# Transposing attention probabilities in halves of 64 query rows, with a reciprocal moved between minima and a store bound set once

## The chip, the core and the metric

The kernel runs on one core of one Trainium2 chip. The metric is the device time of one execution in microseconds (us); lower is better. The core's engines run their own instruction streams and meet at semaphores: TensorE (PE: matmuls, and PEld: its weight loads), VectorE (DVE), ScalarE (ACT), GpSimd (POOL) and SyncE (SP, which issues transfers). TensorE writes to PSUM, eight banks of 512 fp32 values on each of 128 partitions; VectorE and ScalarE copy from there to SBUF.

## The reference

Everything is fp32. `x` is (2, 512, 256), the context (2, 1024, 256). Two gated residual steps:

```
x = x + tanh(g_xattn) * (softmax(mask(q k^T / 8)) v) @ Wo + bo     # q = layernorm(x) @ Wq; k, v = ctx @ Wk, ctx @ Wv
x = x + tanh(g_ffn) * FFN_e(layernorm(x))                          # e = argmax(layernorm(x) @ Wg + bg), 8 experts
FFN_e(t) = gelu(t @ W1[e] + b1[e]) @ W2[e] + b2[e]
```

Attention has 16 heads of 64. `mask` is true on the valid keys of each batch, and the reference puts -max where it is true. So only the last keys of a batch (at most a quarter of 1024) get weight; in this data they fit a window of 160 keys, and the kernel takes that path (`attend_window`).

## The kernel before, in words

For each of the two batches the kernel projects queries and keys, runs the attention loop over the window of 160 keys, projects the result with Wo, normalises again and sorts the rows by expert. Then it runs the experts on chunks of 128 rows, first of batch 0, then of batch 1, and GpSimd stores each chunk with an indirect transfer.

The 160 keys are split into 128 "wide" and 32 "left" ones. The attention loop goes over eight jobs of two units each. A unit `u` is a pair of heads with two tiles of 128 query rows, and has one slot of four in `probs`. What each engine does, in its queue's order, for job `job` of batch `b`:

- TensorE: `scores(2*job+2)` and `scores(2*job+3)` into `s_bank` (in jobs 1 to 6; in job 7 a `fill`, which is other work with 128-row weights), each from 64-row weights, one half of the rows for each head (L1761). Then `values(job-1)`: left keys first (L1799, 64-row weights), then wide ones (L1806, outputs of 64 partitions), accumulated in `o_bank`, columns 0 to 255 of banks 6 and 7. Then `transposes(job)`: eight wide ones into `t_bank` (banks 4 and 5, one for each unit; L1778) and two left ones into bank 7, columns 256 to 511 (L1788), each with 128 query rows.
- VectorE: minima of the scores (`window_max`, four a unit, L1302) for unit 2*job+2, the reciprocal of the sums of unit 2*job+1 (`window_sum`, L1313), minima of unit 2*job+3, the copy of the outputs of job-1 (`job_o`, L1328), the reciprocal of unit 2*job+2, then `job_pT_rest(job)`: copies bank 4 and the left transposes to SBUF (L1323). In some jobs of batch 1 one row tile is normalised for the experts behind that (L1236).
- ScalarE: eight exponentials with sums (`window_exp`, L827) for the two units, then the copy of bank 5 (`job_pT_wide`, L836).
- GpSimd: for each unit the product of the wide probabilities with the reciprocals (L645) and that of the left ones (L647).

The semaphores around it: `ptrans_ready` counts three a job (bank 4, bank 5, left), `pT_dve` and `pT_act` say that the copies are done, `pn_ready` counts GpSimd's products, `o_ready` the values in `o_bank`, `o_dve` VectorE's copy of them. The left transposes wait for `o_dve`, and for `v_dve` in job 0. `head_rows` are partitions 0 to 63 and 64 to 127.

At the end GpSimd's `put_out(g, p)` waits for the result of chunk `p` of batch `g` (`y_taken`, from VectorE's L1251) and issues one store. A flag `over_any` says whether an expert got more rows than two chunks hold; each engine reads it into a register (L704 on GpSimd).

Of the kernel before, what the change touches and what calls it, by code (L numbers as in the profile page):

```python
# [97 lines left out]
def flamingo_kernel(nc, x, ctx_in, mask, g_xattn, g_ffn, wq, wk, wv, wo, bo, wg, bg, w1, b1, w2, b2, out):  # L98
# [38 lines left out]
    with ExitStack() as stack:  # L137
# [231 lines left out]
        left_pT = pT_flat[:, 4 * HALF:5 * HALF]  # L369

# [189 lines left out]
        def _(pool):  # L560
# [59 lines left out]
            out_rows = out.rearrange("b n d -> (b n) d")  # L620

            def put_out(g, p):
# [4 lines left out]
                                             bounds_check=T - 1, oob_is_err=False).then_inc(s_out, 16)  # L627
# [49 lines left out]
            def rest(later_too):  # L677
# [23 lines left out]
                for e in range(E - 1):  # L701
                    put_out(1, e)
                pool.wait_ge(over_ready, 1)
                any_over = pool.value_load(over_any[0:1, 0:1], min_val=0, max_val=1)  # L704
                put_out(1, E - 1)
# [26 lines left out]
        def _(act):  # L732
# [98 lines left out]
            def job_pT_wide(b, job):  # L831

                act.wait_ge(first.ptrans_ready, 3 * (b * JOBS + job) + 2)
                if job >= 1:
                    act.wait_ge(first.o_ready, b * JOBS + job)
                nc.scalar.copy(wide_pT[:, 1].rearrange("p h n -> p (h n)"), bank[5]).then_inc(first.pT_act, 1)  # L836
# [181 lines left out]
        def _(dve):  # L1018
# [272 lines left out]
            def window_max(b, u):  # L1291

                m, j = unit_of(u)
                if u >= PB:

                    dve.wait_ge(first.ptrans_ready, 3 * (b * JOBS + (u - PB) // 2) + 3)
                dve.wait_ge(first.scores_ready, b * PER + (u + 1))
                for i in range(2):
# [17 lines left out]
            def job_pT_rest(b, job):  # L1316

                for part, (dst, src) in enumerate(((wide_pT[:, 0].rearrange("p h n -> p (h n)"), bank[4]),
                                                   (left_pT, bank[7][:, HALF:]))):
                    dve.wait_ge(first.ptrans_ready, 3 * (b * JOBS + job) + 1 + 2 * part)  # L1320
# [18 lines left out]
            def attend_window(b, w, fill, also):  # L1339
# [25 lines left out]
                for job in range(JOBS):  # L1365
                    if 1 <= job < JOBS - 1:
                        window_max(b, 2 * job + 2)
                    if job >= 1:
                        window_sum(b, 2 * job + 1)
                    if 1 <= job < JOBS - 1:  # L1370
                        window_max(b, 2 * job + 3)
# [221 lines left out]
        def _(pe):  # L1593
# [155 lines left out]
            def attend_window(b, fill, also):  # L1749
# [16 lines left out]
                def transposes(job):  # L1766
                    if job >= 1:

                        pe.wait_ge(first.pT_dve, b * PER + 2 * job)
                    for a in range(2):  # L1770
# [3 lines left out]
                        if a == 1 and job >= 1:  # L1774
                            pe.wait_ge(first.pT_act, b * JOBS + job)
                        for i in range(2):
                            for h in range(2):
                                last = nc.tensor.transpose(bank[4 + a][:, h * HALF + i * P:h * HALF + (i + 1) * P],  # L1778
                                                           window_wide(u)[:, 2 * i + h, :], ident[:])
# [441 lines left out]
```

## Time and profile before

| | |
|---|---|
| time, median of 3 runs | 202.68 us (201.56 to 202.85) |
| time of the profiled execution | 201.32 us |
| its span, first to last instruction | 199.5 us |
| mean granted TensorE clock | 0.992 of 2.4 GHz |
| busy: PE / PEld / DVE / ACT / POOL | 96% / 70% / 62% / 53% / 44% |

A matmul's recorded length holds its way through the array, and neighbours overlap; the distance between starts is what one costs. The same holds for VectorE's and ScalarE's rows: the next begins before the recorded end of the one ahead. "issue" is idle time for which the profile has no cause.

### The profile page before, as it was taken

The numbers are of one execution on the slowest core, as the hardware profiler recorded it, in microseconds if no ns is written. First come the engines' busy times: TensorE is split into PE (matmuls) and PEld (weight loads), VectorE is DVE, ScalarE is ACT, GpSimd is POOL, SyncE is SP. The second block draws the span as 40 slices with busy tenths as digits, with TensorE's granted clock in tenths as the row PEclk, the third lists the DMA queues.
The fourth block names the chain that finished last, engine by engine and source line by source line (L and its number), as shares of the span: only waits on it lengthen the run. The fifth ranks groups of instructions, "written<-read, shape, count | busy, mean of one in ns | idle before, by whom it ended". The sixth has DMA issues, their size and how long they took to land.

```text
span 199.5 us, 3974 instructions
## 1 busy us (share of the span) xinstructions
PE 190.5 (96%) x1252; PEld 139.1 (70%) x1252; DVE 123.8 (62%) x538; ACT 105.0 (53%) x376; POOL 88.6 (44%) x128
## 2 busy tenths in 40 slices
PE   7899999999999999999999999999999999999960
PEld 6774364667765544888885667776788889989950
DVE  3479766999896421253459999997924557365520
ACT  3233539799998112211528899998541254345520
POOL 6000005376768991000004898768920014785451
PEclk9999999999999999999999999999999999999996
DMA  5997019999999950570000101500000001353011
GB/s 134 350 367 265 2 37 311 311 320 309 310 323 206 310 168 0 170 250 0 0 5 0 53 30 47 196 3 0 0 3 2 0 0 62 121 159 106 33 33 46
DMA packets 22320, 25.15 MB, mean 126 GB/s; under 512 B 1987, under 2 KB 20877, under 8 KB 22160
## 3 DMA queue, kind: packets, MB, share of 16 engines
q1 hardware_dynamic: 19536, 21.83, 36.9%
q0 software_dynamic: 1152, 2.12, 3.1%
q10 hardware_dynamic: 1600, 0.84, 1.5%
q8 instruction: 13, 0.21, 0.5%
q14 instruction: 19, 0.16, 0.3%
HBM read 14.14 MB, written 11.68 MB: 129 GB/s over the span
## 4 chain that ended last, share of the span: by engine, by line
PE 80%; DVE 9%; DMA 3%; issue 2%; POOL 1%; ACTq 1%; POOLq 0%; ACT 0%; DVEq 0%
PE s_bank L1721 14%; PE o_bank L1666 14%; PE s_bank L1761 8%; PE s_bank L2024 7%; PE t_bank L1778 7%; PE o_bank L1806 7%; PE o_bank L2035 6%; DVE probs L1302 4%; DMA wk_sb<-in_L_xattn_Wk_dram 3%; PE o_bank L1799 3%; PE t_bank L1692 2%; PE s_bank L1833 2%; PE o_bank L1788 2%; PE s_bank L2013 1%; DVE pT L1323 1%
## 5 line engine op out<-in xcount | busy, mean ns | idle before, releaser
L645 POOL TENSOR_TENSOR probs<-probs,r_col 128x512 f32<-128x512 f32 x32 | 33.3, 1040 | 75.1 <-DVE r_col L1313 74.8
L827 ACT ACTIVATE probs<-probs,negm_run 128x160 f32<-128x160 f32 x128 | 53.0, 415 | 8.7 <-DVE negm_run L1302 8.7
L1302 DVE CUSTOM_DVE_ANT_0 probs<-s_bank,maskneg 128x160 f32<-128x160 f32 x128 | 33.3, 317 | 6.1 <-PE s_bank L1761 6.0
L1721 PE MATMUL s_bank<-xnT,wq_sb 128*128 128x512 f32 x64 | 28.8, 597 | 0.0
L1666 PE MATMUL o_bank<-wo_sb,oT 128*128 128x256 f32 x128 | 28.7, 380 | 0.0
L1666 PEld LDWEIGHTS o_bank<-wo_sb,oT 128*128 128x128 f32 x128 | 23.9, 190 | 3.5 <-issue 0.5
L827 ACT ACTIVATION_READ_ACCUMULATOR probs<-probs,negm_run 128x1 f32 x128 | 23.9, 187 | 0.0
L1761 PE MATMUL s_bank<-k_sb,q_sb 64*128 64x160 f32 x256 | 22.3, 311 | 0.0
L1761 PEld LDWEIGHTS s_bank<-k_sb,q_sb 64*128 64x128 f32 x256 | 17.9, 186 | 4.7 <-issue 3.1
L1721 PEld LDWEIGHTS s_bank<-xnT,wq_sb 128*128 128x128 f32 x64 | 11.7, 190 | 13.0 <-issue 12.8
L624 POOL DMA_INDIRECT out_dram<-oT x16 | 16.0, 1001 | 9.3 <-DVE oT L1251 7.5
L1778 PEld LDWEIGHTS t_bank<-ident,probs 128*128 128x128 f32 x128 | 13.5, 141 | 8.0 <-issue 6.2
L1778 PE MATMUL t_bank<-ident,probs 128*128 128x128 f32 x128 | 19.0, 285 | 0.0
L609 POOL DMA_INDIRECT sorted_rows<-rows,place x8 | 8.1, 1006 | 21.2 <-DVE place L1193 19.8
L2024 PE MATMUL s_bank<-k_sb,q_sb 128*128 128x128 f32 x128 | 17.2, 277 | 0.2 <-ACT k_sb L918 0.2
L1806 PE MATMUL o_bank<-pT,v_sb 128*64 128x256 f32 x128 | 17.3, 392 | 0.0
L2024 PEld LDWEIGHTS s_bank<-k_sb,q_sb 128*128 128x128 f32 x128 | 15.7, 192 | 1.0 <-ACT k_sb L918 0.5
L2035 PE MATMUL o_bank<-oT,k_sb 128*128 128x256 f32 x64 | 16.4, 383 | 0.0
L1251 DVE SCALAR_TENSOR_TENSOR oT<-o_bank,gate,oT 128x256 f32<-128x256 f32 x16 | 7.6, 483 | 13.0 <-PE o_bank L2035 13.0
L787 ACT COPY q_sb<-s_bank 128x512 f32<-128x512 f32 x10 | 5.8, 585 | 17.2 <-PE s_bank L1721 14.7
L927 ACT ACTIVATE k_sb<-s_bank,b1T 128x128 f32<-128x128 f32 x32 | 10.0, 364 | 8.8 <-PE s_bank L2024 8.4
L1225 DVE SCALAR_TENSOR_TENSOR rows<-o_bank,gate,rows 128x256 f32<-128x256 f32 x8 | 3.9, 484 | 16.1 <-PE o_bank L1666 16.1
(169 smaller groups left out, 295.6 us busy)
## 6 DMA issues: line engine op xcount, KB each, us to landing
sorted_rows<-empty_row SPq DMA_DIRECT2D x8, 1040.0 KB, 14.5
oT<-in_L_ffn_W_dram SPq DMA_DIRECT2D x1, 2048.0 KB, 18.0
q_sb<-in_L_ffn_W_dram SPq DMA_DIRECT2D x1, 2048.0 KB, 8.4
oT<-sorted_rows SPq DMA_DIRECT2D x1, 1040.0 KB, 5.3
oT<-sorted_rows SPq DMA_DIRECT2D x8, 130.0 KB, 2.2
wq_sb<-in_L_xattn_Wq_dram SPq DMA_DIRECT2D x2, 512.0 KB, 8.0
mask_sb<-in_mask_BxSxS_bk_dram SPq DMA_DIRECT2D x2, 512.0 KB, 8.9
wv_sb<-in_L_xattn_Wv_dram SPq DMA_DIRECT2D x1, 1024.0 KB, 11.0
```

The source lines that it names most:

```text
L624: nc.gpsimd.indirect_dma_start(out=out_rows, in_=srow[g][:, p, 0:D], in_offset=None, out_offset=bass.IndirectOffsetOnAxis(ap=srow[g][:, p, ...
L645: nc.gpsimd.tensor_tensor(window_wide(u), window_wide(u), r.rearrange("p i h -> p (i h)") .unsqueeze(2).broadcast_to([P, 4, WIDE]), ALU.mu ...
L827: last = nc.scalar.activation(window_part(u, i, h), window_part(u, i, h), ACT.Exp, bias=negm_run[at], scale=-1.0, accum_out=l_run[at])
L927: last = nc.scalar.activation(hT[:, p % 2, at], hT_bank(p)[:, at], ACT.Gelu, bias=bias(ic))
L1302: nc.vector.tensor_tensor_reduce(window_part(u, i, h), s_bank[u % 2][:, h, i * CK:i * CK + WK], maskneg[:, q, 0:WK], -SCALE, LARGEST, ALU. ...
L1666: last = nc.tensor.matmul(bank[6 + tt % 2][:, 0:D], oT[:, b, m, q * P:(q + 1) * P], wo_sb[:, m, :], start=(m == 0), stop=(m == M - 1))
L1721: last = nc.tensor.matmul(bank[m % 4], wq_sb[:, c, m * P:(m + 1) * P], xnT[:, c, b * N:(b + 1) * N], start=(c == 0), stop=(c == DC - 1))
L1761: last = nc.tensor.matmul(s_bank[u % 2][:, h, i * CK:i * CK + WK], q_sb[head_rows[h], b, m, q * P:(q + 1) * P], k_sb[head_rows[h], m, 0:WK ...
L1778: last = nc.tensor.transpose(bank[4 + a][:, h * HALF + i * P:h * HALF + (i + 1) * P], window_wide(u)[:, 2 * i + h, :], ident[:])
L1806: last = nc.tensor.matmul(o_bank[head_rows[h], a, 0:HALF], v_sb[:, 0, at * DH:(at + 1) * DH], wide_pT[:, a, h, :], start=False, stop=True)
L2024: last = nc.tensor.matmul(hT_bank(e)[:, ic * P:(ic + 1) * P], w1_sb[:, e, c, ic * P:(ic + 1) * P], sxT[:, e % 2, c * P:(c + 1) * P], start ...
L2035: last = nc.tensor.matmul(bank[6 + p % 2][:, 0:D], hT[:, p % 2, ic * P:(ic + 1) * P], weights(ic), start=(ic == 0), stop=(ic == IC - 1))
```

## The change

Every transpose of 128 query rows becomes two of 64 (`head_rows[r]`), the halves taking turns. The first half's result goes to bank 4 and the second half's to bank 5, for both units of the job; the left ones go to banks 6 and 7. The copies to SBUF put the halves back into the old order, so `values` reads what it read before. `ptrans_ready` now counts two a job (all wide, left), and VectorE's first copy waits for all wide transposes. The wait for ScalarE's copy stands ahead of the wide values, and ahead of the whole of the next transposes, instead of in the middle of either. In jobs 1 to 6 the reciprocal of unit 2*job+1 goes between the two tiles of unit 2*job+2. GpSimd's `put_out` takes its bound from a register set once, where an integer had made one register move for each store, and reads `over_any` between stores 4 and 5 of batch 1 and not ahead of the last one.

```diff
+        wide_of_row_half = wide_pT.rearrange("p a h (i r n) -> p r (a h i) n", i=2, r=2)
+        left_of_row_half = left_pT.rearrange("p (i r n) -> p r i n", i=2, r=2)
...
+            last_row = pool.alloc_register("pool_last_row")
+            pool.reg_mov(last_row, T - 1)
...
-                                             bounds_check=T - 1, oob_is_err=False).then_inc(s_out, 16)
+                                             bounds_check=last_row, oob_is_err=False).then_inc(s_out, 16)
...
-                for e in range(E - 1):
+                for e in range(E // 2):
                     put_out(1, e)
                 pool.wait_ge(over_ready, 1)
                 any_over = pool.value_load(over_any[0:1, 0:1], min_val=0, max_val=1)
-                put_out(1, E - 1)
+                for e in range(E // 2, E):
+                    put_out(1, e)
...
-                act.wait_ge(first.ptrans_ready, 3 * (b * JOBS + job) + 2)
+                act.wait_ge(first.ptrans_ready, 2 * (b * JOBS + job) + 1)
...
-                nc.scalar.copy(wide_pT[:, 1].rearrange("p h n -> p (h n)"), bank[5]).then_inc(first.pT_act, 1)
+                nc.scalar.copy(wide_of_row_half[:, 1], bank[5].rearrange("p (u n) -> p u n", n=DH)).then_inc(first.pT_act, 1)
...
-                for part, (dst, src) in enumerate(((wide_pT[:, 0].rearrange("p h n -> p (h n)"), bank[4]),
-                                                   (left_pT, bank[7][:, HALF:]))):
-                    dve.wait_ge(first.ptrans_ready, 3 * (b * JOBS + job) + 1 + 2 * part)
+                for part, (dst, src) in enumerate((
+                        (wide_of_row_half[:, 0], bank[4].rearrange("p (u n) -> p u n", n=DH)),
+                        (left_of_row_half, o_bank[:, :, HALF:HALF + P].rearrange("p r (i n) -> p r i n", i=2)))):
+                    dve.wait_ge(first.ptrans_ready, 2 * (b * JOBS + job) + 1 + part)
...
                     if 1 <= job < JOBS - 1:
-                        window_max(b, 2 * job + 2)
+                        window_max(b, 2 * job + 2, (0,))
                     if job >= 1:
                         window_sum(b, 2 * job + 1)
                     if 1 <= job < JOBS - 1:
+                        window_max(b, 2 * job + 2, (1,))
                         window_max(b, 2 * job + 3)
...
                         pe.wait_ge(first.pT_dve, b * PER + 2 * job)
+                        pe.wait_ge(first.pT_act, b * JOBS + job)
                     for a in range(2):
                         u = 2 * job + a
 
                         pe.wait_ge(first.pn_ready, 2 * (g + u) + 1)
-                        if a == 1 and job >= 1:
-                            pe.wait_ge(first.pT_act, b * JOBS + job)
                         for i in range(2):
                             for h in range(2):
-                                last = nc.tensor.transpose(bank[4 + a][:, h * HALF + i * P:h * HALF + (i + 1) * P],
-                                                           window_wide(u)[:, 2 * i + h, :], ident[:])
-                        last.then_inc(first.ptrans_ready, 1)
+                                at = (4 * a + 2 * h + i) * DH
+                                for r in range(2):
+                                    last = nc.tensor.transpose(bank[4 + r][:, at:at + DH],
+                                                               window_wide(u)[head_rows[r], 2 * i + h, :],
+                                                               ident[head_rows[r], head_rows[r]])
+                    last.then_inc(first.ptrans_ready, 1)
...
                     for i in range(2):
-                        last = nc.tensor.transpose(bank[7][:, HALF + i * P:HALF + (i + 1) * P], left_probs[:, job % 2, i, :],
-                                                   ident[:])
+                        for r in range(2):
+                            last = nc.tensor.transpose(o_bank[:, r, HALF + i * DH:HALF + (i + 1) * DH],
+                                                       left_probs[head_rows[r], job % 2, i, :],
+                                                       ident[head_rows[r], head_rows[r]])
                     last.then_inc(first.ptrans_ready, 1)
...
+                    pe.wait_ge(first.pT_act, b * JOBS + (job + 1))
                     for a in range(2):
-                        if a == 1:
-                            pe.wait_ge(first.pT_act, b * JOBS + (job + 1))
```

## Rows read from the trace of the kernel before

**Rows 1.** The page: shares of the chain that ended last, by engine

```profile
PE 80%; DVE 9%; DMA 3%; issue 2%; POOL 1%; ACTq 1%; POOLq 0%; ACT 0%; DVEq 0%
```

**Rows 2.** Windows view, two periods: us, then busy us (instructions) of PE, PEld, DVE, ACT, POOL

```profile
41.63:45.74 4.11, 4.11 (x39) 2.91 (x39) 3.71 (x22) 3.87 (x19) 2.80 (x5) 1.00 1.09 315
...
129.86:133.96 4.10, 4.10 (x42) 2.91 (x41) 4.06 (x22) 3.87 (x18) 2.83 (x5) 1.00 0.02 4
```

**Rows 3.** Waits of 36 to 62 us: total us, times, longest

```profile
DVE probs L1302 <- PE s_bank L1761: 2.4, 6, 0.4
...
PEld s_bank L1761 <- issue: 1.0, 6, 0.2
```

**Rows 4.** Timeline of weight loads: start us, length, line, tiles, shape, count, idle before

```profile
43.35 0.63 PEld L1806 LDWEIGHTS o_bank<-pT,v_sb 128*64 128x64 f32 x8 [0.33 <-issue]
44.37 0.42 PEld L1778 LDWEIGHTS t_bank<-ident,probs 128*128 128x128 f32 x4 [0.39 <-issue]
44.93 0.42 PEld L1778 LDWEIGHTS t_bank<-ident,probs 128*128 128x128 f32 x4
45.37 0.20 PEld L1788 LDWEIGHTS o_bank<-ident,pT 128*128 128x128 f32 x2
45.74 0.57 PEld L1761 LDWEIGHTS s_bank<-k_sb,q_sb 64*128 64x128 f32 x8 [0.17 <-issue]
```

**Rows 5.** Timeline of the matmuls there, then L1761 and L1778: min/median/max ns

```profile
45.43 0.38 PE L1788 MATMUL o_bank<-ident,pT 128*128 128x128 f32 x2
...
L1761 PE MATMUL s_bank<-k_sb,q_sb x256: 296/296/400, 28.5 to 134.1; 64*128 64x160 f32 x128
...
L1778 PE MATMUL t_bank<-ident,probs x128: 272/273/332, 36.1 to 140.2; 128*128 128x128 f32 x128
```

**Rows 6.** Timeline of VectorE in that job

```profile
42.60 0.33 DVE L1302 CUSTOM_DVE_ANT_0 probs<-s_bank,maskneg 128x160 f32<-128x160 f32 x1 [0.40 <-PE s_bank L1761]
...
43.59 0.17 DVE L1313 RECIPROCAL r_col<-l_run 128x4 f32<-128x4 f32 x1
...
44.63 0.69 DVE L1328 COPY oT<-o_bank 128x512 f32<-128x512 f32 x1
...
45.32 0.66 DVE L1323 COPY pT<-t_bank 128x512 f32<-128x512 f32 x1
45.89 0.41 DVE L1323 COPY pT<-o_bank 128x256 f32<-128x256 f32 x1
```

**Rows 7.** Timeline of GpSimd, then of ScalarE, in that job

```profile
43.84 1.04 POOL L645 TENSOR_TENSOR probs<-probs,r_col 128x512 f32<-128x512 f32 x1 [1.07 <-DVE r_col L1313]
44.84 0.40 POOL L647 TENSOR_TENSOR pT<-probs,r_col 128x128 f32<-128x128 f32 x1
...
42.42 0.56 ACT L836 COPY pT<-t_bank 128x512 f32<-128x512 f32 x1
43.22 0.43 ACT L827 ACTIVATE probs<-probs,negm_run 128x160 f32<-128x160 f32 x1 [0.24 <-DVE negm_run L1302]
```

**Rows 8.** Timeline of matmuls behind job 6's transposes, batch 0

```profile
61.85 0.38 PE L1788 MATMUL o_bank<-ident,pT 128*128 128x128 f32 x2
62.07 1.02 PE L1721 MATMUL s_bank<-xnT,wq_sb 128*128 128x512 f32 x2
```

**Rows 9.** Timeline of weight loads behind job 6, batch 1

```profile
137.72 0.30 PEld L1799 LDWEIGHTS o_bank<-pT,v_sb 64*128 64x128 f32 x4 [0.35 <-DVE pT L1323]
```

**Rows 10.** Timeline of GpSimd's stores

```profile
171.81 0.99 POOL L624 DMA_INDIRECT out_dram<-oT  x1 [0.30 <-issue]
...
193.26 0.98 POOL L624 DMA_INDIRECT out_dram<-oT  x1 [0.77 <-DVE oT L1251]
194.55 0.98 POOL L624 DMA_INDIRECT out_dram<-oT  x1 [0.31 <-issue]
```

**Rows 11.** Timeline of 64-row loads, window ended within 0.02 and within 0.12 us

```profile
65.60 0.19 PEld L1799 LDWEIGHTS o_bank<-pT,v_sb 64*128 64x128 f32 x2 [0.76 <-issue]
...
65.60 0.30 PEld L1799 LDWEIGHTS o_bank<-pT,v_sb 64*128 64x128 f32 x4 [0.76 <-issue]
```

More of the change, by code:

```diff
@@ L1289, in take_o, with window_max @@
                 nc.vector.tensor_copy(*o_dst(slot, u)).then_inc(S.o_dve, 1)
-            def window_max(b, u):
+            def window_max(b, u, tiles=(0, 1)):
                 m, j = unit_of(u)
[L1294 to L1298, printed above, removed]
+                if tiles[0] == 0:
+                    if u >= PB:
+                        dve.wait_ge(first.ptrans_ready, 2 * (b * JOBS + (u - PB) // 2) + 2)
+                    dve.wait_ge(first.scores_ready, b * PER + (u + 1))
+                for i in tiles:
                     q = 2 * j + i
```

## The prediction

> **What bounds the kernel now.** I read the page first: TensorE is recorded as busy for 96% of the span, and it holds 80% of the chain that ended last [rows 1]. That does not yet say that TensorE's own work sets the pace, since a matmul's recorded end is modelled. So I took the attention loop apart, the part that the change touches. The windows view, cut at the start of two jobs, gives a period of 4.11 us in batch 0 and 4.10 us in batch 1; VectorE is busy 3.71 us of it in batch 0 and 4.06 us in batch 1, ScalarE 3.87 us in both [rows 2]. The waits of batch 0's stretch name two things that recur once in each of six jobs: VectorE waits 0.4 us for the next scores, and TensorE's weight loads for the scores sit idle about 0.17 us for nothing that the profile can name ("issue") [rows 3].
>
> Then the timeline, to close the loop. VectorE starts its minima at 42.60, eight of them and a reciprocal, then copies the outputs from 44.63 to 45.32 [rows 6]. The left transposes wait for that copy: their load starts at 45.37 [rows 4], their matmuls at 45.43 and, 0.11 later, 45.54 (0.38 less one length of 0.27) [rows 5]. The scores' first load starts only at 45.74 [rows 4], and its matmul is recorded 0.40 long where the others take 0.30, so it really begins near 45.84 [rows 5]. The next minima start one period on, at 46.71. The sum: 2.72 + 0.05 + 0.06 + 0.11 + 0.30 + 0.87 = 4.11 us, all of the period. This loop (VectorE's minima and output copy, left transposes, scores) is the bound in batch 0. Its one piece in which nobody works is the 0.30 between the last left transpose and the first scores matmul.
>
> A second loop is almost as long. GpSimd's wide product starts 0.08 after the reciprocal and ends at 44.88; the fifth wide transpose load starts at 44.93. It costs 0.13 us: the first wide matmul follows its load (44.37) by 0.06 as the left one does, at 44.43, the first left matmul is at 45.43, and eight of them 0.11 apart would need 0.87. The left product ends at 45.24, just before VectorE's copy at 45.32 [rows 4 to 7]. Without the 0.13 TensorE would reach the left transposes at 45.30 and wait for VectorE all the same.
>
> **Part 1, the transposes in halves.** Before: ten single transposes a job, each a load of 128 x 128 and a matmul of 128 columns, one every 0.11 us [rows 4, 5]. After: twenty with 64 rows and 64 columns, the two row halves taking turns. The trace shows no transpose of 64 rows, but it shows loads of that tile shape: two start in the same hundredth of a microsecond, the next two 0.11 later [rows 11]. I take that: a pair of half transposes costs what one whole one cost, 0.11 us, and the phase keeps its length. The bound from below is a little less than nothing added (matmuls of half the columns); from above, two loads one behind the other, 10 x 0.11 = 1.1 us more a job. I choose the lower end because the rows are of the same tile shape.
>
> What goes is the change of tile shape ahead of the scores, which use 64-row tiles already. Where two 128-row forms follow each other, as at the end of batch 0, the next matmul begins at 62.07, 0.11 after the last left transpose (61.85 + 0.38 - 0.27 = 61.96) [rows 8]. Against 0.30 that is 0.19 us saved. This lies on the bounding loop, and it occurs six times a batch [rows 3].
>
> The same change of shape now appears where transposes are followed by 128-row work, after jobs 6 and 7 of each batch: instead of 0.11 the gap is 0.30 less the 0.05 that the shorter matmul saves, 0.25; that is +0.14 us each.
>
> The Trainium skill bears on this in two places, and nothing below needs it. "TensorEngine Tiling (Array Packing)", Key Properties, says that changing the tiling mode drains the array; the idle 0.17 us before the scores agrees. "TensorE: Matmul & The Clock Gate", LDWEIGHTS, says that a load's time goes by its columns and not its rows, which speaks against halves: twice the loads at the old price each, unless the two row groups overlap. By that sentence alone the kernel would be the slow rival below; the two loads that start together [rows 11] are why I don't follow it.
>
> **Part 2, fewer signals.** VectorE's wide copy used to wait for the first bank only, and started at 45.32, right behind the output copy [rows 6]. Now it waits for all wide transposes. Without GpSimd's delay the eighth pair begins at 44.37 + 0.06 + 7 x 0.11 = 45.20 and ends near 45.42 (0.27 less 0.05 for the shorter matmul); with 0.04 to 0.15 for the signal the copy starts at 45.46 to 45.57, so VectorE gains a wait of 0.14 to 0.25 us. Behind it in its queue are the left copy and the next minima. VectorE would be free at 45.89 + 0.33 + the wait = 46.36 to 46.47; the shortened period asks for the minima at 42.60 + 3.92 = 46.52. So in the plain jobs the old idle 0.40 covers it, with 0.05 to 0.16 to spare; without that cover it costs up to 0.25 a job. ScalarE's copy already waited for both banks. The values' wait for that copy moves ahead of all wide matmuls, by half of them, and the copy ends at 42.98, 0.37 before even the first one's load at 43.35 [rows 4, 7]; nothing.
>
> Part 2 costs where VectorE is full: the jobs of batch 1 that also normalise a row tile (L1236) ahead of new minima; two do, behind jobs 4 and 5. Their period of 4.10 has 4.06 busy [rows 2]. I give these two transitions a gain of 0.05 each instead of 0.19. And after job 6 of batch 1 the value matmuls wait for VectorE's left copy [rows 9], so the new wait goes straight to the end: +0.20.
>
> **Part 3, the reciprocal between the minima.** It moves from behind the fourth minimum to behind the second, about 0.49 us earlier (four minima take 43.59 - 42.60 = 0.99) [rows 6], so GpSimd's products end 0.49 earlier and the fifth transpose's 0.13 us goes. ScalarE starts at 43.22 on the first two minima [rows 7], which start when they did; the third and fourth come 0.1 later and ScalarE reaches them 0.8 later. VectorE's total work is the same. By itself this is worth nothing, because the output copy (45.32) and not GpSimd's left product (45.24) releases the left transposes; what it does is to take away the cover that would have made Part 2 worse.
>
> **Part 4, GpSimd's stores.** The bound register is set once in place of sixteen times, and the read of the overflow flag moves between store 4 and store 5. The last two stores start 1.29 us apart, and the last one's idle 0.31 [rows 10] is what back-to-back stores have anyway (0.30 at 171.81). The read must then be over within that idle and the store ahead of it. So nothing is late because of it: 0, at best -0.05 from the register move on the way to the last stores. In the middle of the list GpSimd waits for results, which hides the read.
>
> **The sum.** Batch 0: -6 x 0.19 + 2 x 0.14 = -0.86. Batch 1: -4 x 0.19 - 2 x 0.05 + 0.20 + 0.14 = -0.52. The new gap behind job 6 in batch 1 lies beside the wait just counted. Stores: -0.03. Together -1.4 us. What follows the attention is a stream of matmuls, so the shift reaches the end. The profiled run has a span of 199.5 and a time of 201.32, the median of the runs is 202.68: a new span of 198.1, a profiled time of 199.9, and a median of 201.3.
>
> **Rivals.** First, slower: the half transposes don't overlap. TensorE itself then takes 3.79 us (4.11 less 0.13 less 0.19) plus 10 times what a pair costs beyond 0.11. The break-even with 4.11 is 0.14 us a pair (0.32 over ten), 0.035 us for each of its four instructions; at the full 0.22 it is 3.79 + 1.1 = 4.9 a period, so about 12 x 0.8 + 4 x 1.1 = +14 us, 216.7; at 0.16, 12 x 0.18 + 4 x 0.5 = +4, 206.9. Against it: [rows 11]. For it: no such transpose is in the trace. Chance 0.10.
>
> Second, no gain from the shape: the idle before the scores is tied to the handover and stays. Then 12 x 0.19 and the 0.14s fall away, VectorE's later wide copy is left, +0.2 after job 6 and up to 0.15 in the full jobs: +0.5, 203.2. For it: the row says "issue", not a cause. Against it: [rows 8]. Chance 0.10.
>
> Third, VectorE's new wait takes the gain: the signal takes longer than 0.15, and the plain jobs end at 4.0 instead of 3.92. Then 10 x 0.1 goes back and 0.2 in the full ones: -0.2 to -0.6, about 202.2. Chance 0.15.
>
> Fourth, more gain: the smaller loads shorten the left transposes too and the period falls to what ScalarE needs, 3.87 [rows 2]. 10 x 0.05 more and 0.2 from the missing stall after job 6: -2.1, 200.6. Chance 0.13.
>
> My forecast holds the other 0.52.
>
> **How the numbers follow.** 1% of 202.68 is 2.0 us, about what a measurement of this kernel can tell from no change. Faster by more than that needs under 200.65: half of the fourth rival and, as medians of this kernel's runs move by half a microsecond, a quarter of the forecast: 0.22. Slower by over 1%: the first rival, 0.10, and a little of the second: 0.12. The rest, 0.66, is within. The range goes from the fourth rival less a little, 200.2, to the second, 203.3; what lies outside is the first rival and the tails.
>
> **What would show it.** Right: the idle before the scores' loads (six a batch) gone, half transposes in pairs 0.11 apart, a period near 3.92 in the plain jobs and 4.05 in the full ones, VectorE's wait for scores under 0.1 and a new wait of about 0.2 at its wide copy. Wrong: loads of the halves one behind another; the 0.17 still there; a wait at the wide copy above 0.3; the last two stores closer than 1.29.

## The result and the profile after

The kernel after takes 200.08 us (median of 4 runs, 199.73 to 200.14) against 202.40 us of the kernel before (4 runs, 201.56 to 202.85). The ratio is 0.989, with a 95% interval of 0.986 to 0.992. I had forecast 201.3 us and a range of 200.2 to 203.3: the time lies just below the range, and the gain is 2.3 us where I had worked out 1.4. The profiled run took 200.14 us, with a span of 198.28 us.

The span is only 1.20 us shorter than before, since the first minima start 1.04 us later (30.50 against 29.46). Apart from one register move on GpSimd, the changed lines come after that point, and in the runs below the start lies anywhere from 29.8 to 30.7 us; the 30.7 belongs to a kernel whose attention takes as long as before (the second run). So I compare stretches between two events of the attention. The start of a job is that of its first wide transpose load, read from the timelines:

| stretch | before | after | forecast | measured |
|---|---|---|---|---|
| first minima to job 0, batch 0 | 6.63 | 6.63 | 0 | 0 |
| batch 0, job 0 to job 7 | 31.15 | 29.79 | -1.00 | -1.36 |
| job 7 of batch 0 to job 0 of batch 1 | 43.54 | 43.63 | +0.14 | +0.09 |
| batch 1, job 0 to job 7 | 28.58 | 27.48 | -0.66 | -1.10 |
| job 7 of batch 1 to the end | 60.11 | 60.25 | +0.11 | +0.14 |
| sum | | | -1.4 | -2.2 |

The sum agrees with the medians. The last row carries no weight: that stretch takes between 59.94 and 60.25 us in all runs but the twelfth, so that its +0.14 is within its scatter. The other four repeat within 0.02 us between kernels with the same attention. The periods of single jobs are these: in batch 0, before, 4.17, five of 4.11 (one reads 4.10) and 6.45; after, 3.93, five of 3.86 and 6.55. In batch 1, before, 4.41, five of 4.11 (one reads 4.10) and 3.64; after, 4.16, four of 3.86 or 3.87, 3.97 and 3.90.

The page, shares of the chain that ended last, which answers to [rows 1], and its lines:

```profile
PE 69%; DVE 21%; issue 3%; ACT 2%; POOL 1%; POOLq 1%; DVEq 0%
PE s_bank L1729 14%; PE o_bank L1674 14%; DVE probs L1308 12%; PE s_bank L2035 8%; PE o_bank L2046 7%; PE s_bank L1769 5%; DVE oT L1335 4%; PE s_bank L1608 3%; PE s_bank L1639 2%; PE o_bank L1817 2%; PE o_bank L1799 2%; PE t_bank L1700 2%; PE s_bank L1844 2%; ACT probs L832 2%; PE s_bank L2024 1%
```

VectorE has gone from 9% to 21%, by its minima (L1308) and its output copy (L1335): in batch 0 the chain now leaves TensorE in every job and comes back through them, where before it stayed on TensorE from job to job.

Windows of two periods, as in [rows 2], a plain job of batch 0 and one of batch 1 that also normalises a row tile; the columns are us, then busy us (instructions) of PE, PEld, DVE, ACT and POOL:

```profile
43.17:47.03 3.86, 3.57 (x52) 2.58 (x51) 3.70 (x22) 3.86 (x19) 2.79 (x5) 1.00 1.09 293
128.53:132.50 3.97, 3.58 (x52) 2.58 (x52) 3.97 (x24) 3.88 (x19) 2.84 (x5) 1.00 0.00 0
```

TensorE, busy for the whole period before, now has 0.3 us free in 3.86. VectorE has no free time in the job that normalises, and ScalarE's recorded busy time fills the plain one (what that is worth, the seventh run shows).

Waits of 37 to 62 us, the stretch of [rows 3]; total us, times, longest:

```profile
PEld o_bank L1799 <- DVE oT L1335: 2.6, 6, 0.4
...
PEld o_bank L1817 <- ACT pT L841: 1.7, 5, 0.3
...
DVE probs L1308 <- PE s_bank L1769: 1.0, 6, 0.2
```

The row of the scores' loads that sat idle for "issue" is gone. VectorE's wait for the scores fell from 0.4 to 0.16 us a job. New is TensorE's own wait of 0.4 us for the output copy, ahead of the left transposes: the wide ones are done so much sooner that it stands there idle. The row that names ScalarE's copy (L1817 <- L841) is new in name only in these jobs: the loads of the wide values sat idle for 0.33 us before as well, for "issue" [rows 4]. There is no row for VectorE's wide copy (L1330), where I had forecast a wait of about 0.2.

The timelines of one job, of TensorE's loads, then of its matmuls, then of VectorE, as in [rows 4 to 6]:

```profile
44.92 0.58 PEld L1787 LDWEIGHTS t_bank<-ident,probs 64*128 64x128 f32 x16 [0.38 <-issue]
45.93 0.20 PEld L1799 LDWEIGHTS o_bank<-ident,pT 64*128 64x128 f32 x4 [0.43 <-DVE oT L1335]
46.05 1.12 PEld L1769 LDWEIGHTS s_bank<-k_sb,q_sb 64*128 64x128 f32 x16
```

```profile
44.93 0.72 PE L1787 MATMUL t_bank<-ident,probs 64*128 64x64 f32 x16
45.93 0.34 PE L1799 MATMUL o_bank<-ident,pT 64*128 64x64 f32 x4 [0.29 <-DVE oT L1335]
46.11 0.63 PE L1769 MATMUL s_bank<-k_sb,q_sb 64*128 64x160 f32 x6
```

```profile
43.17 0.32 DVE L1308 CUSTOM_DVE_ANT_0 probs<-s_bank,maskneg 128x160 f32<-128x160 f32 x1 [0.16 <-PE s_bank L1769]
...
45.19 0.69 DVE L1335 COPY oT<-o_bank 128x512 f32<-128x512 f32 x1
45.80 0.17 DVE L1319 RECIPROCAL r_col<-l_run 128x4 f32<-128x4 f32 x1
45.88 0.66 DVE L1330 COPY pT<-t_bank 128x512 f32<-128x512 f32 x1
46.46 0.41 DVE L1330 COPY pT<-o_bank 128x256 f32<-128x256 f32 x1
47.03 0.33 DVE L1308 CUSTOM_DVE_ANT_0 probs<-s_bank,maskneg 128x160 f32<-128x160 f32 x1 [0.16 <-PE s_bank L1769]
```

Sixteen half loads take 0.58 us and one is 0.14 long (median 0.139), so eight pairs start (0.58 - 0.14) / 7 = 0.063 us apart. Before, eight whole ones went every 0.11. The wide copy runs right behind the reciprocal.

The loop adds up as before. From the minima (43.17) to the end of the output copy (45.88) 2.71; 0.05 to the left load (45.93); 0.06 to its matmul (45.99; the row has 45.93, but this first record is 0.05 us longer than the ones behind it, as the scores' first one was before, and I take its start later by that). The minima at 47.03 follow the first scores matmul by the old 0.87, so that one is at 46.16, 0.17 behind the first left transpose. 2.71 + 0.05 + 0.06 + 0.17 + 0.87 = 3.86. Only the handover from the first left transpose to the scores differs: 0.11 + 0.30 = 0.41 before, 0.17 after, where I had forecast 0.22.

The last two stores, which answer to [rows 10]:

```profile
191.49 0.98 POOL L628 DMA_INDIRECT out_dram<-oT  x1 [0.77 <-DVE oT L1256]
192.78 0.98 POOL L628 DMA_INDIRECT out_dram<-oT  x1 [0.30 <-issue]
```

They are still 1.29 us apart. The step behind job 6 of batch 1, in the chain of waits:

```profile
136.00 0.50 ACT probs L832 x3
136.50 0.48 ACT pT L841
136.98 0.04 issue
137.02 1.11 PE o_bank L1817 x8
```

This job's period is 3.90 against 3.64 before. I had forecast that the value matmuls would wait for VectorE's left copy there, as in [rows 9]; the last release is ScalarE's copy of bank 5, whose wait the change has put ahead of all wide value matmuls (the seventh run shows how much of the 0.26 that is).

### The profile page after: what moved, and what is told of

Its sections match the earlier page's. It is cut to its first block, busy times and chain, and to the rows that moved or that the text cites. A ratio compares the mean times of both kernels' runs of the same rounds, so it can differ in the third digit from the quotient of the medians.

```text
span 198.3 us, 4265 instructions
## 1 busy us (share of the span) xinstructions
PE 185.5 (94%) x1412; PEld 136.2 (69%) x1412; DVE 123.5 (62%) x538; ACT 104.9 (53%) x376; POOL 89.5 (45%) x128
## 4 chain that ended last, share of the span: by engine, by line
PE 69%; DVE 21%; issue 3%; ACT 2%; POOL 1%; POOLq 1%; DVEq 0%
PE s_bank L1729 14%; PE o_bank L1674 14%; DVE probs L1308 12%; PE s_bank L2035 8%; PE o_bank L2046 7%; PE s_bank L1769 5%; DVE oT L1335 4%; PE s_bank L1608 3%; PE s_bank L1639 2%; PE o_bank L1817 2%; PE o_bank L1799 2%; PE t_bank L1700 2%; PE s_bank L1844 2%; ACT probs L832 2%; PE s_bank L2024 1%
## 5 line engine op out<-in xcount | busy, mean ns | idle before, releaser
L1308 DVE CUSTOM_DVE_ANT_0 probs<-s_bank,maskneg 128x160 f32<-128x160 f32 x128 | 33.3, 317 | 3.5 <-PE s_bank L1769 3.2
L1769 PE MATMUL s_bank<-k_sb,q_sb 64*128 64x160 f32 x256 | 21.7, 306 | 0.0
L628 POOL DMA_INDIRECT out_dram<-oT x16 | 17.0, 1064 | 7.8 <-DVE oT L1256 5.9
L1817 PE MATMUL o_bank<-pT,v_sb 128*64 128x256 f32 x128 | 17.3, 392 | 0.1
L1787 PEld LDWEIGHTS t_bank<-ident,probs 64*128 64x128 f32 x256 | 9.5, 139 | 6.5 <-issue 6.2
L1335 DVE COPY oT<-o_bank 128x512 f32<-128x512 f32 x16 | 11.0, 686 | 3.9 <-PE o_bank L1817 3.9
```

Source lines behind the costliest of these rows:

```text
L628: nc.gpsimd.indirect_dma_start(out=out_rows, in_=srow[g][:, p, 0:D], in_offset=None, out_offset=bass.IndirectOffsetOnAxis(ap=srow[g][:, p, ...
L1308: nc.vector.tensor_tensor_reduce(window_part(u, i, h), s_bank[u % 2][:, h, i * CK:i * CK + WK], maskneg[:, q, 0:WK], -SCALE, LARGEST, ALU. ...
L1335: nc.vector.tensor_copy(oT[:, b, 2 * quad:2 * quad + 2, j * HALF:(j + 1) * HALF], o_bank[:, :, 0:HALF]).then_inc(first.o_dve, 1)
L1769: last = nc.tensor.matmul(s_bank[u % 2][:, h, i * CK:i * CK + WK], q_sb[head_rows[h], b, m, q * P:(q + 1) * P], k_sb[head_rows[h], m, 0:WK ...
L1817: last = nc.tensor.matmul(o_bank[head_rows[h], a, 0:HALF], v_sb[:, 0, at * DH:(at + 1) * DH], wide_pT[:, a, h, :], start=False, stop=True)
```

## The experiments

Times are medians, each against the kernel before run in the same series on the same chip (its medians there were 201.99 to 202.06); in brackets stands the 95% interval of the ratio. "Attention" is the time from the first minima to the start of job 7 of batch 1: 109.91 us before, 107.53 after.

**The stores alone** (the kernel before, with this part only):

```
+            last_row = pool.alloc_register("pool_last_row")
+            pool.reg_mov(last_row, T - 1)
...
-                                             bounds_check=T - 1, oob_is_err=False).then_inc(s_out, 16)
+                                             bounds_check=last_row, oob_is_err=False).then_inc(s_out, 16)
...
-                for e in range(E - 1):
+                for e in range(E // 2):
...
-                put_out(1, E - 1)
+                for e in range(E // 2, E):
+                    put_out(1, e)
```

> Only GpSimd's part of the change (bound register set once, flag read between stores 4 and 5). Theory A (the whole gain comes from cheaper transposes and the missing change of tile shape in the attention loop): no measurable difference, 0 to -0.05 us; the last two stores still start 1.29 us apart. Rival B (the flag read held up the last store): -0.3 us, last two stores closer than 1.2 us.

202.13 us, 1.0007 [0.9986, 1.0027]; attention 109.92; the last two stores still start 1.29 us apart. The stores bring nothing that can be measured.

**The reciprocal alone** (the kernel before, with this part only):

```
-                        window_max(b, 2 * job + 2)
+                        window_max(b, 2 * job + 2, (0,))
                     if job >= 1:
                         window_sum(b, 2 * job + 1)
                     if 1 <= job < JOBS - 1:
+                        window_max(b, 2 * job + 2, (1,))
                         window_max(b, 2 * job + 3)
```

> Only the reciprocal moved between the minima, whole transposes kept. Theory A: the period of the plain jobs stays 4.10 to 4.11 us, because VectorE's output copy and not GpSimd's product releases the left transposes; 0 to -0.1 us in all. The fifth wide transpose no longer waits. Rival B (GpSimd's late product was part of the bound): period 3.98, -1.3 us.

202.44 us, 1.0013 [0.9989, 1.0037]; attention 109.90, every period as before. The fifth transpose's wait for GpSimd's product is gone and nothing is won: it wasn't on the loop.

**The halves alone** (the change without the two parts above):

> Only the transposes in halves; reciprocal and stores as before. Theory A: pairs of half transposes 0.06 us apart; the fifth pair still waits for GpSimd, VectorE's wide copy then waits some 0.15 us for it, period 3.87 to 3.92 us, -1.7 to -2.2 us in all. Rival B (the reciprocal carries a large part): period 4.0, about -1.2 us.

200.75 us, 0.9936 [0.9912, 0.9961]; attention 108.45. Batch 0 has the periods of the kernel after within 0.02 (3.86 to 3.88), but batch 1 has 3.95, 3.95, 4.33 and 4.25 among its seven. Waits of 111 to 138 us, then GpSimd's and the loads' timelines in one of its jobs:

```profile
PEld t_bank L1783 <- POOL probs L647: 2.5, 6, 0.7
```

```profile
134.27 1.04 POOL L647 TENSOR_TENSOR probs<-probs,r_col 128x512 f32<-128x512 f32 x1 [1.29 <-DVE r_col L1316]
```

```profile
135.36 0.33 PEld L1783 LDWEIGHTS t_bank<-ident,probs 64*128 64x128 f32 x8 [0.69 <-POOL probs L647]
```

The second half of the wide transposes starts 0.05 us after GpSimd's late product ends (134.27 + 1.04 = 135.31), and VectorE's wide copy and the normalisation queue up behind them. In the kernel after that row of waits is 0.2 us in all.

**The halves and the reciprocal** (the change without the stores):

> Halves and reciprocal, stores as before. Theory A: the same as the changed kernel within 0.1 us, period 3.86, -2.3 us. Rival B (the stores carry 0.3): -2.0 us.

199.76 us, 0.9892 [0.9862, 0.9923]; attention 107.56, the periods of the kernel after. So the reciprocal is worth 0.89 us of attention (108.45 to 107.56) with the halves and nothing without them.

**One row group at a time** (the kernel after; the lower 64 rows in a block of four behind the upper ones):

```
-                        for i in range(2):
-                            for h in range(2):
-                                at = (4 * a + 2 * h + i) * DH
-                                for r in range(2):
+                        for r in range(2):
+                            for i in range(2):
+                                for h in range(2):
+                                    at = (4 * a + 2 * h + i) * DH
```

> The changed kernel, but the wide half transposes run four times on the upper rows and then four times on the lower rows, instead of taking turns. Theory A (a half transpose costs half by its 64 columns and its short load, 0.06 us, and the two row groups run at the same time when they take turns): single ones 0.06 apart, wide phase 16 x 0.06 = 0.98 us instead of 0.49; VectorE's wide copy then waits, period about 3.95 to 4.05. Rival B (the gain in pace comes from the short matmul alone, the row groups do not overlap): pace and period as in the changed kernel, 3.86.

199.90 us, 0.9898 [0.9858, 0.9939]; attention 107.53, the periods unchanged, which is not what I had expected of the phase. The order in the program does not decide this question. In the trace the loads and matmuls of the two blocks lie beside each other all the same. The timeline of matmuls shows 16 in little more than the 0.72 of the kernel after:

```profile
44.67 0.76 PE L1787 MATMUL t_bank<-ident,probs 64*128 64x64 f32 x16
```

What a half costs is settled by the tenth and twelfth runs.

**The left transposes whole** (the kernel after, with only the left ones and their copy as before):

```
-                        for r in range(2):
-                            last = nc.tensor.transpose(o_bank[:, r, HALF + i * DH:HALF + (i + 1) * DH],
-                                                       left_probs[head_rows[r], job % 2, i, :],
-                                                       ident[head_rows[r], head_rows[r]])
+                        last = nc.tensor.transpose(bank[7][:, HALF + i * P:HALF + (i + 1) * P], left_probs[:, job % 2, i, :],
+                                                   ident[:])
```

> The changed kernel, but the two left transposes a job stay whole, with 128 rows, so the change of tile shape ahead of the scores is back. Theory A: the idle 0.17 us before the scores' loads is back and the loop through VectorE's output copy grows by 0.19 to 0.25 us: period 4.05 to 4.11, most of the gain gone. Rival B (the gain is the quicker wide phase, the left transposes do not matter): period 3.86 to 3.90.

202.41 us, 1.0017 [0.9994, 1.0040]; attention 110.04, the plain periods 4.10 and 4.11. All of the gain is gone, with eight of ten transposes still in halves. Its timeline of weight loads has the old idle time ahead of the scores again:

```profile
46.37 0.20 PEld L1798 LDWEIGHTS o_bank<-ident,pT 128*128 128x128 f32 x2 [0.43 <-DVE oT L1335]
46.74 0.57 PEld L1769 LDWEIGHTS s_bank<-k_sb,q_sb 64*128 64x128 f32 x8 [0.17 <-issue]
```

This kernel has one more change of tile shape than the one before, ahead of the left transposes. It costs nothing that the rows show: TensorE waits there for the output copy, and the load starts 0.05 us behind it as always. So while the left transposes are whole, halves of the wide ones are worth nothing; the left ones are the group on the loop.

**Less work for ScalarE** (the kernel after; ScalarE copies half of bank 5 and the other half of its probabilities is left out, so the output is not the reference's):

```
-                nc.scalar.copy(wide_of_row_half[:, 1], bank[5].rearrange("p (u n) -> p u n", n=DH))
+                nc.scalar.copy(wide_of_row_half[:, 1, 0:4], bank[5][:, 0:HALF].rearrange("p (u n) -> p u n", n=DH))
```

> The changed kernel, ScalarE copies only half of its bank of transposed probabilities (the other half is left out, so the attention output is not the reference's), 0.2 us less work for it a job. Theory A (the loop through VectorE's output copy is as long as ScalarE's work, both 3.86): period stays 3.86. Rival B (ScalarE alone is the bound now): period 3.7 to 3.75, another -1 us in all.

199.29 us, 0.9875 [0.9833, 0.9916]; attention 107.37. The periods stay 3.86, so ScalarE does not set them, although the windows view of the kernel after has it busy for 3.86 of 3.86 (here it is 3.66). The last period of batch 1 falls from 3.90 to 3.75: there ScalarE's copy is on the chain.

**The left transposes later** (the kernel after; they stand behind the next job's first unit of scores, so that the scores no longer wait for VectorE's output copy):

```
-                    if job >= 1:
+                def left_transposes(job):
+                    if job >= 1:
...
                         scores(2 * job + 2)
+                        left_transposes(job - 1)
                         scores(2 * job + 3)
                     elif job == JOBS - 1:
+                        left_transposes(job - 1)
                         fill(0)
...
+                left_transposes(JOBS - 1)
                 fill(1)
```

> The changed kernel, the left transposes go behind the next job's first unit of scores, so the scores no longer wait for VectorE's output copy. Theory A (two bounds of 3.86): period stays 3.86 since ScalarE is busy all the time. Rival B (VectorE's loop alone is the bound now): period 3.75, another -1 us in all.

199.08 us, 0.9863 [0.9833, 0.9893]; attention 106.70. Batch 0 falls to 3.71, 3.75 and four of 3.78; batch 1 is at 27.47 as a whole, as in the kernel after. I had expected that ScalarE's 3.86 would hold the period, and it didn't: after the change it was VectorE's loop alone (the rival said 3.75; the eleventh run shows what holds 3.78). This is the fastest version with the reference's output, though its interval overlaps that of the kernel after.

**The wide transposes whole** (the kernel after, with only the wide ones and their two copies as before):

```
-                                at = (4 * a + 2 * h + i) * DH
-                                for r in range(2):
-                                    last = nc.tensor.transpose(bank[4 + r][:, at:at + DH],
-                                                               window_wide(u)[head_rows[r], 2 * i + h, :],
-                                                               ident[head_rows[r], head_rows[r]])
+                                last = nc.tensor.transpose(bank[4 + a][:, h * HALF + i * P:h * HALF + (i + 1) * P],
+                                                           window_wide(u)[:, 2 * i + h, :], ident[:])
```

> The kernel after, but with the wide transposes as whole ones of 128 rows (eight a job, into banks 4 and 5 by units as before, with the copies of before), while the left transposes stay in halves. Theory A: the gain comes through the left transposes and the scores behind them, and the halves of the wide transposes are worth something only where VectorE is close to waiting for them. Whole ones go every 0.11 us, so that the eight take 0.87 us in place of 0.49 and VectorE's copy of the wide ones, which ran right behind the reciprocal, waits some 0.1 to 0.2 us. The copy of the output ends later by that, so a period is near 3.95 in place of 3.86, the time 200.6 to 201.8 (ratio 0.992 to 0.997), and VectorE's wait for the wide transposes stands in the waits with about 0.1 to 0.2 us each. Theory B: the left halves are all of it; the period stays 3.86 and the time at 200.0.

200.41 us, 0.9916 [0.9883, 0.9948]; attention 108.27. The period is 3.88, between the two theories. The wait forecast for VectorE's wide copy is there: the copy starts 0.26 us after the reciprocal where it starts 0.08 after it in the kernel after (about 0.09 us of it is idle, and the waits have no row for it, where I had expected one). VectorE's timeline:

```profile
45.90 0.17 DVE L1319 RECIPROCAL r_col<-l_run 128x4 f32<-128x4 f32 x1
46.16 0.69 DVE L1330 COPY pT<-t_bank 128x512 f32<-128x512 f32 x1
46.77 0.41 DVE L1330 COPY pT<-o_bank 128x256 f32<-128x256 f32 x1
47.15 0.33 DVE L1308 CUSTOM_DVE_ANT_0 probs<-s_bank,maskneg 128x160 f32<-128x160 f32 x1
```

Of these 0.18 us 0.16 fall into the time in which VectorE waits for the scores anyway; 0.02 are left. In batch 1 one period is 4.32 where the kernel after has 3.97. So the halves of the wide transposes are worth 0.7 us of attention, half of it in that one job, which I have not followed further.

**The upper wide halves twice** (24 half transposes a job in place of 16):

```
-                                for r in range(2):
+                                for r in (0, 0, 1):
                                     last = nc.tensor.transpose(bank[4 + r][:, at:at + DH],
```

> The kernel after, with each wide half transpose of the upper 64 rows issued twice (24 half transposes a job in place of 16; the second writes the same values again). Theory A: each half of TensorE's rows takes its own half transposes, one in 0.06 us, beside the other half's. Then the 16 upper ones take 16 x 0.06 = 0.98 us, the lower eight lie inside that, VectorE's copy of the wide ones waits some 0.1 to 0.3 us, and the period is 4.0 to 4.1. Theory B: a half transpose costs 0.03 us wherever it goes; 24 take 0.74 us, the wide ones are done about 0.25 us later than in the kernel after, which is about when the reciprocal ends, and the period stays within 0.03 of 3.86.

201.58 us, 0.9981 [0.9958, 1.0005]; attention 109.07, periods 3.98. Its matmuls, then VectorE's wide copy:

```profile
44.40 1.15 PE L1787 MATMUL t_bank<-ident,probs 64*128 64x64 f32 x23
...
45.39 0.22 PE L1787 MATMUL t_bank<-ident,probs 64*128 64x64 f32 x1
```

```profile
45.66 0.69 DVE L1330 COPY pT<-t_bank 128x512 f32<-128x512 f32 x1 [0.26 <-PE t_bank L1787]
```

The last starts 0.99 us after the first. The first record is 0.05 longer than the others again, and the other 0.94 are fifteen steps of 0.063 between sixteen upper ones, with the eight lower ones inside. Each half of the rows is a lane of its own, with a half transpose every 0.06 us, as Theory A has it (its period of 4.0 to 4.1 came out as 3.98); the second theory's 0.74 is out.

**Both loops shortened** (the left transposes later, as above, and ScalarE's copy halved with the other half of its probabilities left out):

> The left transposes stand behind the next job's first unit of scores, and ScalarE copies only half of bank 5 (the other half of that bank's probabilities is left out, so the output is not the reference's). With the left transposes alone moved the periods of batch 0 were 3.78. Theory A: those 3.78 are ScalarE's (eight exponentials of 0.41 and a copy of 0.47, one behind the other). With 0.17 us less of copy the period falls to 3.65 or less in batch 0, until VectorE's own work of 3.57 to 3.6 holds it; batch 1 stays near 3.9 to 3.95, as GpSimd's 1.9 us a job and the chain through its second product set it. Time 197.9 to 198.7. Theory B: the 3.78 are VectorE's, which waits for the left transposes there; the period stays within 0.03 of 3.78 and the time at 199.1 or a little under.

198.11 us, 0.9798 [0.9772, 0.9824]; attention 105.85. Windows of one period, first of the run with the left transposes later, then of this one:

```profile
44.40:48.18 3.78, 3.67 (x50) 2.58 (x48) 3.78 (x22) 3.78 (x19) 2.84 (x5) 1.00 1.09 324
```

```profile
44.32:47.93 3.61, 3.61 (x51) 2.58 (x49) 3.61 (x24) 3.61 (x19) 2.80 (x5) 1.00 1.08 299
```

The period falls by 0.17, what the shorter copy was meant to bring: at 3.78 ScalarE held the period, while at 3.86 the same cut had brought nothing. Batch 1 stays at 3.93 to 3.97 in six of its seven periods, as expected. At 3.61 VectorE's rows follow one another without a gap and ScalarE's record is full too; which of the two holds that period is not tested.

**The upper left halves twice** (six half transposes a job in place of four):

```
-                        for r in range(2):
+                        for r in (0, 0, 1):
                             last = nc.tensor.transpose(o_bank[:, r, HALF + i * DH:HALF + (i + 1) * DH],
```

> The kernel after, with the two left half transposes of the upper 64 rows issued twice (six half transposes a job in place of four; the second writes the same values again). It puts a price on the pair of half transposes where they stand on the chain that sets the period: output copy, left transposes, scores, minima. Theory A: each half of the rows takes a half transpose in 0.06 us beside the other's, so two more upper ones make the path 2 x 0.06 = 0.12 us longer and a period 3.98 in place of 3.86; 12 such periods give 1.4 us, the time 201.4. Theory B, the price in the prediction: a pair goes every 0.11 us, so two more would add 0.22 us and the period would be 4.08, the time 202.4. Theory C: 0.03 us for each half transpose whatever its rows: a period of 3.92, the time 200.7.

The periods are 3.99, and attention 109.08: two more on the loop cost 0.13 us, as Theory A has it, and not the 0.22 of my price. The time, though, is 203.22 us, 1.0060 [1.0040, 1.0081], which no theory foresaw: attention explains 1.55 us over the kernel after, and 2.5 us more come at the end. TensorE's sequencer, at the branch that skips the overflow path, first here and then in the kernel after (duration min/median/max in ns, first and last start):

```profile
L2174 PEldq COMPARE_BRANCH  x1: 3671/3671/3671, 192.5 to 192.5; - x1
```

```profile
L2174 PEldq COMPARE_BRANCH  x1: 357/357/357, 191.1 to 191.1; - x1
```

In all the other kernels this branch takes 0.36 or 0.37 us. The next one, L2198, takes 4.7 to 5.4 us in every kernel; here it ends 3.3 us after GpSimd's last instruction and so sets the end.

## Why the prediction was off

**The bounding loop** was the right one, and its sum holds after as before, term by term.

**Part 1 failed in one term: "a pair of half transposes costs what one whole one cost, 0.11 us".** It costs 0.06. I had the price from two 64-row loads 0.11 apart [rows 11], but those belong to matmuls of 256 columns. My own rows held the better sign. Two whole transposes' loads together take 0.20 us [rows 4], and one is 0.14 long, so these loads stand 0.06 apart; their matmuls stand 0.11 apart [rows 5]. By these rows it was the matmul of 128 columns that paced a transpose, not its load, and a half transpose has 64 columns. (Whether the load or the matmul paces a half no run separates: both follow one another every 0.06.) I called this bound "a little less than nothing added" and gave it no size: 0.05 us on the loop, and 8 x 0.05 in the wide phase. The twelfth run puts the pair at 0.06 on the loop, the tenth in the wide phase. Of the 0.8 us that I missed, 0.5 to 0.6 are this term at the ten handovers that I had at 0.19, and 0.3 the two full jobs (under Part 2).

The Trainium skill ("TensorE: Matmul & The Clock Gate", LDWEIGHTS) puts a load's time at its columns over 1.2 GHz, an estimate of 0.107 us for 128 columns. The traces do not agree for these transposes: the half loads of one lane start 0.062 apart, with 128 columns each.

**The idle time from the change of tile shape** is worth the 0.19 us that I gave it: of the 0.24 saved, 0.05 is the pace. The sixth run gives both back together, so this split rests on the timelines: the first scores matmul now begins 0.11 behind the last left transpose (46.16 against 46.05), and 0.30 before. The price in the other direction was too high, 0.10 and 0.09 us where transposes in halves are now followed by 128-row work in batch 0, against 0.14.

**Part 2, fewer signals.** The forecast wait of VectorE's wide copy did not come, because the phase took 8 x 0.06 in place of 8 x 0.11. With the phase at its old length, in the ninth run, the wait is 0.18, inside my 0.14 to 0.25, and hidden in the plain jobs as I had it. Through this the gain in the full jobs was undersized: -0.24 and -0.14 in place of -0.05 each. Behind job 6 of batch 1 the size was near (+0.26 against +0.20), but by luck, since the cause was another: ScalarE's copy. I had called the wait moved ahead of the wide value matmuls "nothing" from a plain job where that copy was long done; the seventh run, with a shorter copy, takes 0.15 of the 0.26 back. The other 0.11 is not explained.

**Part 3, the reciprocal**, is worth nothing alone, as forecast. I said that it takes away the cover that would make Part 2 worse, and gave no size; the halves without it lose 0.89 us, all of it in batch 1.

**Part 4, the stores:** nothing, as forecast.

**The rivals.** The fourth, with 200.6, was nearest, at a chance of 0.13. Its shorter left transposes came true, and its period of 3.87 too, but this not for its reason, "what ScalarE needs": the seventh run cuts ScalarE's work and no plain period moves, and in the eighth ScalarE does the same work in 3.78. VectorE's loop and ScalarE's recorded time met by chance. The stall behind job 6 that it left out was there. The other three are out: the halves overlap, the idle time went, and VectorE's wait did not come. (The chance that I gave for a gain of over 1% adds up wrongly: half of 0.13 and a quarter of 0.52 are 0.20, not 0.22.)

## What to carry to other kernels

Before pricing a new form from the nearest rows, see which of its two instructions paces the old one: put the distance of the loads and that of the matmuls side by side, and scale the one that is longer. In a loop with several engines a shorter step is worth something only where it stands on the chain. Making eight of the ten transposes nearly twice as fast was worth 0.7 us beside faster left ones, and nothing without them: the two behind the output copy decided whether there was a gain at all. A busy share of 100% does not make an engine the bound; halving one of its operations, and seeing whether the period moves, does tell.

## What was not expected of the hardware

- The two halves of TensorE's rows take their half transposes side by side even when the program issues four for one half and then four for the other: 16 matmuls in 0.76 us against 0.72. The records don't name the half; with one half transpose every 0.06 us in a half (the tenth run), sixteen one behind the other would take about 1 us.
- ScalarE's records fill the period at 4.11 to within 0.24, and at 3.86, 3.78 and 3.61 wholly; at 3.86 it was not the bound, at 3.78 it was. So slack can lie inside its recorded durations: behind the copy of about 0.56 us the next exponential starts 0.56 later in the kernel after, and 0.47 in the eighth run.
- A branch on TensorE at the end of the program took 0.36 us in thirteen kernels and 3.67 us in one with 32 more transposes, while one with 128 more showed nothing. The Trainium skill ("Runtime: NRT & Kernel Launch", Instruction fetch mechanics) says that a taken branch whose target is not in the sequencer's two pages of instructions waits for their transfer. The long branch agrees with it; no run here moved the code alone, so it stays a likely cause and is not shown.
